# VectorE's order in the first half of a step, and one more activation on ScalarE per step

## What is computed

```python
def _layer(x, wqkv, qs, ksc, wo, lg, lb, w1, b1, w2, b2):
    h = shift_token(x)
    q, k, v = split(h @ wqkv)            # 8 heads of 64
    q = l2norm(q) * qs
    k = l2norm(k) * ksc
    q, k = rotary_xpos(q, k)             # q*cos + rotate_half(q)*sin, the same for k
    o = local_attention(q, k, v)         # windows of 128 rows: own and previous window
    x = x + o @ wo
    h = shift_token(x)
    h = layernorm(h) * lg + lb
    a, g = split(h @ w1 + b1)            # 682 columns each
    h = a * gelu(g)
    return x + h @ w2 + b2
```

## Time and profile before

| what | value |
|---|---|
| median of 3 runs | 873.93 us (873.52 to 874.31) |
| the profiled execution, its own time | 871.19 us |
| its span | 869.4 us |
| TensorE busy | 740.1 us (85%) |
| VectorE busy | 526.7 us (61%) |
| ScalarE busy | 486.9 us (56%) |
| GpSimd busy | 422.7 us (49%) |
| mean granted TensorE clock | 0.956 |

### The profile page before, as it was taken

The page is one execution under the profiler, slowest core; times in us unless marked ns, Lnnn a source line. Parts: engine busy times, 40 slices in busy tenths (PEclk is TensorE's granted clock), DMA queues, the critical chain, the costliest instruction groups (busy, mean ns, idle before and its releaser), DMA issues.

```text
span 869.4 us, 17037 instructions
## 1 busy us (share of the span) xinstructions
PE 740.1 (85%) x4984; PEld 615.9 (71%) x4984; DVE 526.7 (61%) x1469; ACT 486.9 (56%) x1273; POOL 422.7 (49%) x592
## 2 busy tenths in 40 slices
PE   5888768989898989898988898898989898989867
PEld 5777646767676777777776777677767676777747
DVE  2899883665556565656565637565666556565732
ACT  2343425575657565756566655756575657565642
POOL 0433453664536364645362646545464636453622
PEclk9999887899999999999999988999999999999998
DMA  7444314421010101010101001010101010101000
GB/s 223 143 134 136 94 41 146 149 71 38 2 37 0 36 0 36 0 36 0 36 0 37 1 1 49 2 48 0 48 0 48 0 48 0 48 0 37 1 25 12
DMA packets 32786, 38.36 MB, mean 44 GB/s; under 512 B 8476, under 2 KB 22896, under 8 KB 32752
## 3 DMA queue, kind: packets, MB, share of 16 engines
q1 hardware_dynamic: 32752, 37.95, 13.6%
HBM read 29.55 MB, written 8.39 MB: 44 GB/s over the span
## 4 chain that ended last, share of the span: by engine, by line
PE 49%; DVE 16%; ACT 13%; issue 12%; POOL 5%; DMA 3%; DVEq 1%; SPq 1%; ACTq 0%; POOLq 0%
PE ps L420 32%; ACT pr L852 4%; PE ps L619 3%; PE ps L596 3%; PE ps L578 2%; DVE turned L1116 2%; DMA arena<-x 2%; ACT L822 2%; DVE arena L950 2%; PE ps L515 1%; PE ps L590 1%; PE ps L413 1%; POOL xrs L1270 1%; PE ps L623 1%; ACT pT L858 1%
## 5 line engine op out<-in xcount | busy, mean ns | idle before, releaser
L1352 POOL TENSOR_SCALAR pr<-pr,rl 128x128 f32<-128x128 f32 (+1 forms) x256 | 107.5, 433 | 80.5 <-DVE rl L1154 80.3
L852 ACT ACTIVATE pr<-sm,mn 128x128 f32<-128x128 f32 (+1 forms) x256 | 113.3, 445 | 20.4 <-DVE mn L1148 19.9
L420 PE MATMUL ps<-hT_hi,w_hi 128*128 128x256 f32 (+1 forms) x352 | 106.5, 302 | 1.4 <-DVE hT_lo L1120 1.4
L1148 DVE CUSTOM_DVE_ANT_0 sm<-ps,wmask 128x128 f32<-128x128 f32 (+1 forms) x256 | 80.0, 354 | 44.1 <-PE ps L596 38.7
L420 PE MATMUL ps<-hT_lo,w_hi 128*128 128x256 f32 (+1 forms) x352 | 102.7, 292 | 0.0
L420 PE MATMUL ps<-hT_hi,w_lo 128*128 128x256 f32 (+1 forms) x352 | 102.4, 291 | 0.0
L1334 POOL TENSOR_TENSOR u_lo<-u_pair,u_hi 128x256 fp32r<-128x256 f32 x64 | 67.3, 1059 | 69.1 <-ACT u_hi L831 67.0
L1323 POOL TENSOR_TENSOR rn<-ss,nhalf 128x16 f32<-128x16 f32 x32 | 93.6, 2926 | 2.7
L420 PE MATMUL ps<-wqkv_hi,yT_hi 128*128 128x512 f32 x192 | 79.8, 416 | 13.6 <-DVE arena L992 6.0
L810 ACT ACTIVATE sqb<-ps 128x512 f32<-128x512 f32 x64 | 38.0, 595 | 94.2 <-PE ps L420 86.7
L578 PE MATMUL ps<-ident,turned 128*128 128x128 f32 x256 | 41.0, 300 | 43.7 <-DVE turned L1116 43.7
(11 more groups left out here) (146 smaller groups left out, 2092.1 us busy)
## 6 DMA issues: line engine op xcount, KB each, us to landing
arena<-x SPq DMA_DIRECT2D x16, 256.0 KB, 3.3
ystream<-arena SPq DMA_DIRECT2D x16, 256.0 KB, 2.0
y_next<-ystream SPq DMA_DIRECT2D x16, 256.0 KB, 2.7
y_res<-ystream SPq DMA_DIRECT2D x16, 256.0 KB, 2.6
arena<-L_ffn_w SPq DMA_DIRECT2D x6, 640.0 KB
arena<-ctx SPq DMA_DIRECT2D x8, 256.0 KB, 3.7
arena<-mask_BxSxS_ik SPq DMA_DIRECT2D x8, 256.0 KB, 2.7
xmid<-arena SPq DMA_DIRECT2D x8, 256.0 KB, 2.0
```

The lines of the kernel that those rows point to most:

```text
L420: last = mm(out, lhsT(a), rhs(b), start=(start and i == 0), stop=(stop and i == 2))
L852: A(pr[:, h % NS, a:b], sm[:, h % NS, a:b], ACT.Exp, bias=mn[:, h, t:t + 1], scale=-1.0, accum_out=ls[:, h, t:t + 1]).then_inc(e_done, 1)
L1148: V.tensor_tensor_reduce(sm[:, h % NS, a:b], bank(h % SB)[:, a:b], wmask[:, a:b], 1.0, -NEG, ALU.add, ALU.min, mn[:, h, t:t + 1]).then_inc ...
L1352: G.tensor_scalar(pr[:, h % NS, a:b], pr[:, h % NS, a:b], rl[:, h, t:t + 1], 1.0, ALU.mult, ALU.mult).then_inc(pn_done, 1)
```

## The change

VectorE's list for the first half of a step gets another order: `add_queries(0)` and the two norms of tile 1 move ahead of `low_hT`, and `scale_heads(0)` moves from behind the sine part of tile 1 to directly behind `low_hT`, ahead of the cosine part of tile 1. ScalarE gets one more activation per step with a feed-forward part: a Gelu of one column of a small tile, `table_touch`, directly behind hT_hi. The tile is set to 0 by VectorE at the start, and ScalarE waits for that once.

```diff
+        table_touch = sb("table_touch", [P, 2])
...
+        touch_set = sem("touch_set")
...
             def between(b):
                 if b == 1:
                     A(tg[:], g_in[:], ACT.Tanh).then_inc(tanh_done, 1)
+                    act.wait_ge(touch_set, 1)
...
                     A(hT[0][:], halves(7), ACT.Copy).then_inc(hT_high, 1)
+                    A(table_touch[:, 1:2], table_touch[:, 0:1], ACT.Gelu)
                 if la is not None:
                     values(1)
...
             V.memset(nhalf[:], -0.5).then_inc(nhalf_set, 1)
+            V.memset(table_touch[:], 0.0).then_inc(touch_set, 1)
...
                 if A:
                     rotate_cos(0)
                     rotate_sin(0)
+                    add_queries(0)
+                    norms(1, 0)
+                    norms(1, 1)
                 if F:
                     low_hT()
                 if A:
-                    norms(1, 0)
-                    norms(1, 1)
-                    add_queries(0)
+                    scale_heads(0)
                     rotate_cos(1)
                 if F:
                     gated(0)
                 if A:
                     rotate_sin(1)
-                    scale_heads(0)
                 if F:
                     gated(1)
```

## The result

The changed kernel takes 823.07 us (median of 4 runs, 822.57 to 824.24), the kernel before beside it 873.72; the ratio is 0.943, 95% interval 0.941 to 0.944. That is 50.7 us less, where 45.0 were forecast. The two profiled executions are closer to the sum: 871.19 and 824.24, 46.95 apart; the first is the lowest of its kernel, the second the highest.

The account below looks back on a forecast made before the run. Bound: TensorE's idle time before the transposes, waiting for `scale_heads(0)`, and its lower clock afterwards. Sum: 34.3 + 2.0 + 9.4 - 0.75 = 45.0 us, so 873.93 becomes 828.9; range 821 to 841, the forecast's own 824 to 834.

Parts of the forecast that it names:

- The bound and the place: TensorE, busy 85%, idles before the transposes of line 578, which wait for `scale_heads(0)`: 43.7 us in 17 waits.
- The new times of VectorE: Step 10's new VectorE schedule, summed from trace rows, less 0.08 per joint, with 0.14 per hand-over.
- The pause, 2.45 a step: TensorE's idle time before tile 0's transposes goes: 2.45 in each of 14 steps, 34.3 us; step 9 gives 2.0.
- the delay of `up(0)`: `low_hT` ends 0.19 later, so `up(0)` on TensorE starts 0.13 later per step, bounds 0 and 0.3.
- The clock, 7 x 1.34: Without the pause TensorE's clock no longer falls to 1.2 GHz behind it in seven steps: 9.4 us gained.
- the start: Step 0, without `up` work: `scale_heads(0)` waits for the key sum and a hand-over is exposed; about 0.75 us lost.
- The touch, priced at 0 with -0.2 to +0.3: ScalarE's gelu table loads earlier, but VectorE reaches `gated(0)` no sooner: worth 0 per step, bounds -0.2 and +0.3 us.
- the cover is the one microsecond that `gated(0)` has in hand: Reason for the zero price: a shift of the first gelu by tenths would not make TensorE wait for `gated(0)`.
- The wait that moves on to `up(5)`: TensorE stops at `up(4)` or `up(5)`, with 0.45 and 0.2 in hand, for 0.8 us a step: 841 us; 10%.
- The clock that falls all the same: TensorE's clock still falls, at the attention half's earlier waits: 838 us, or 849 with a fall every step; 7%.
- The blocked query sum: `add_queries(0)` on VectorE must wait for GpSimd's power of line 1323, 1.33 later per step: 849 us; 3%.
- rival 3: `add_queries(0)` on VectorE is blocked by GpSimd's power until 581.90, delaying `low_hT` and `up(0)`: 849 us; 3%.

Follow-up runs that it names:

- a pause made on purpose: The changed kernel with `scale_heads(0)` moved behind `gated(0)`: 835.25 us beside 872.47 of the kernel before, ratio 0.957.
- The filled pause: The kernel before with 20 additional matmuls, their result overwritten, on TensorE before the transposes of tile 0: 863.25 us beside 872.47, ratio 0.988.
- cosine part first: The changed kernel with tile 1's cosine part ahead of `scale_heads(0)`, and the old order in step 0: 820.7 us beside 821.68 of the changed kernel.
- the run with GpSimd's low parts held back: The changed kernel without the touch, GpSimd's low parts of the gated rows waiting for tile 1's scaling: 821.06 us beside 872.0 of the kernel before, ratio 0.941.
- the filling alone: The changed kernel with `scale_heads(0)` back behind the sine part, sums and norms early, touch kept: 871.67 us beside 872.47 of the kernel before.

## Why the prediction was right, and where it was not

- **The bound and the place.** Right: the transposes waited for the place of `scale_heads(0)` in VectorE's list. Moved alone it brings about half of the gain, and a pause made on purpose costs 1.08 per step where 1.07 was worked out.
- **The new times of VectorE.** With 26.02 added, the trace after has `low_hT` at 582.26 (said: 582.36), the scaling of tile 0 at 583.19 (583.25), `gated(0)` at 585.47 (585.6), the end of `gated(1)` at 587.53 (587.7). Adding up rows with 0.08 for each joint and 0.14 for each hand-over was good to 0.2 us.
- **The pause, 2.45 a step.** Mis-sized: 2.77. Steps of 43.6 became 40.8. Of the missing 0.32, 0.13 is the delay of `up(0)`, which did not come, and 0.17 is the overlap of a matmul with the one behind it: 2.59 is counted from a modelled end at 586.20, while a following matmul would have started 0.17 earlier. Over steps 1 to 6 and 9 to 15 the sum comes to 12 x 2.45 + 2.0 + 6 x 1.34 = 39.4, and the traces show 43.4.
- **The clock, 7 x 1.34.** Right in kind, and 0.09 short in size per fall, since it was read over the transposes and `up` only. The filled pause measured 9.2 us for it. That the sum's 9.4 comes so near is in part luck, as the seven falls are those of one execution (see the point on the 5.7 us).
- **Steps 7 to 9 and the start.** The span is 47.0 shorter. From the first `low_hT` to the last it is 47.75, the start lost 1.0 (said: 0.75), and the end gained 0.3. Of the start only step 0's own chain can be held against the sum: it lost 0.76, while the first `low_hT` comes 2.3 us apart in two traces of one and the same kernel (169.26 and 171.53, cosine part first). Steps 7 to 9 gained 4.3, where the sum has 2 x 2.45 + 1.34 = 6.2: step 7 to 8 brought only 1.5, because a fall of the clock came that was not there before. The same pattern at the start of step 8 is shown by TensorE's timeline and a window of 1 us, first of the kernel before, then of the changed one:

```profile
472.91 0.47 PE L420 MATMUL ps<-wqkv_hi,yT_hi 128*128 128x512 f32 x1 [2.56 <-DVE wqkv_lo L1029]
```

```profile
475.00:476.00 1.00, 1.00 (x7) 0.82 (x7) 1.00 (x2) 0.19 (x1) 0.00 (x0) 1.00 0.00 0
```

```profile
450.81 0.47 PE L422 MATMUL ps<-wqkv_hi,yT_hi 128*128 128x512 f32 x1 [2.56 <-DVE wqkv_lo L1034]
```

```profile
453.00:454.00 1.00, 1.00 (x6) 0.90 (x6) 1.00 (x2) 0.12 (x1) 0.00 (x0) 0.50 0.00 0
```

It is the same pause of 2.56, once without and once with a fall. The changed kernel's other profiled run (821.44 us) had no fall there. This is about 1 us of the scatter between runs.
- **The 5.7 us between 45.0 and 50.7.** The two profiled executions account for 2.0 of them, as above. The other 3.7 lie in which executions were profiled: that of the kernel before is 2.5 below its median, that of the changed kernel 1.2 above. The first has a visible cause. Its mean granted clock is 0.956, where 35 further executions of that kernel, beside the experiments, have 0.946 to 0.958 with a median of 0.950; among these, one that lost 1 us more to the clock (span times 1 - clock) took about 0.8 us longer. A clock lower by 0.006 over 872 us is 5.2 us of full speed, so by estimate up to three falls of 1.7 more than the seven, at 1.43 us of time each. So `7 x 1.34` fits one fast execution, and the median of the kernel before had more to gain. No trace shows where those falls were, so this stays an estimate. The 1.2 us of the changed kernel stay open: its four executions have 0.961 to 0.964, and the profiled one has the highest.
- **The touch, priced at 0 with -0.2 to +0.3.** Wrong: 0.56 in a regular step, 6.3 us by the traces and 8.9 by the medians. The step that failed is "the cover is the one microsecond that `gated(0)` has in hand". That cover holds for TensorE's wait for `gated(0)`, and the run with GpSimd's low parts held back shows it. What I did not ask is which GpSimd instruction starts just ahead of VectorE's when VectorE comes 0.27 us later. The price came from an engine that was in none of my terms for this part.
- **The rivals.** The wait that moves on to `up(5)` (10%) did not come with the full change; it came with half of it, at the size of 0.3 to 0.6 us. The clock that falls all the same (7%) fell once more in one step. The blocked query sum (3%) was tested by the change itself: line 1106 ran at 554.44 inside the power of 552.95 to 555.88 and took 0.69, as always (691 to 693 ns in all 16).

The rule cited with rival 3, from the Trainium skill, "SBUF — State Buffer", section "SBUF: two separate sides" (a VectorE instruction with two SBUF inputs and a GpSimd instruction that reads SBUF exclude each other, and the first one keeps the other out), is borne out by the low parts: 0.74 against 1.74 us, and 1.22 against 1.68, by who came first. It holds for the power where VectorE is first (3.70 to 3.98 us instead of 2.93). It does not hold where the power is first: VectorE ran beside it at full speed.

## What to carry to other kernels

When an engine with an ordered list holds up another, find the instruction that ends the wait and put it ahead of everything that nobody waits for yet; fill idle time in front of a late operand with work that is already possible, but expect nothing from the filling alone (0.999 here). Before pricing a shift of some tenths of a microsecond at nothing, look at which GpSimd instruction starts within these tenths beside a two-input VectorE instruction, and let the engine with time to spare come second. A pause of TensorE has two prices, its length and, after some pauses, the clock behind it; filling it with idle matmuls measured the second one alone. The price of the clock differs between executions of one kernel, so compare the mean granted clock of all of them before counting falls in one trace.

## What the runs showed of the hardware that was not expected

- The granted clock does not follow from the length of the last pause. In steps of the same work, a pause of 2.58 us was followed by a fall in 7 of 14 steps (and the 2.10 of step 9 by none), one of 2.44 in 9 of 14, one of 2.08 in 10 of 15, one of 0.89 in none of 15, each count from one trace. The pause of 2.56 at the start of step 8 was followed by a fall in one execution of the changed kernel and by none in another. Each fall behind these pauses was to 1.2 GHz and took 1.7 us of full speed by the windows, 1.4 to 1.5 us in a step's length. What decides whether it comes stays open.
- GpSimd's power of 128x16 takes 2.92 or 2.93 us in every run, also with a two-input VectorE instruction inside it, unless it starts during such an instruction: then it takes 3.70 (118.69 in step 0 of the changed kernel, behind line 1121 from 118.33) to 3.98 (570.89 with the scaling moved alone, behind line 1116 from 570.87). The small multiplication ahead of it took 1.31 instead of 0.28 where it started during line 1121. So the wait is paid when the instruction starts; that this is where it reads its inputs is a guess.
